# A cross-attention and quantized feed-forward kernel: a first pass over all batches, gate arithmetic on 128 partitions, decay exponents by one matmul of four heads, another order of attention and weight units

## The reference

```python
x = x + mlstm(layernorm(x), ctx, ctx, Wi, bi, Wf, bf, ln_scale)
x = x + ffn(layernorm(x), w_gate, w_up, w_down)
# mlstm, for each batch and head
log_f_cum = cumsum(log_sigmoid(fg)); log_D = tril(log_f_cum[s] - log_f_cum[t]) + ig[t]
D = exp(log_D - max_t log_D); C = (q @ k.T) / sqrt(32) * D
n = maximum(abs(C.sum(-1)), exp(-max_log_D)); h = (C / (n + EPS)) @ v
hn = (h - mean(h)) * rsqrt(var(h) + EPS) * ln_scale
# ffn: every operand quantized (_q_act to 3 mantissa bits, _q_w to 1, shared power of two per 32)
inter = silu(q_act(x) @ q_w(w_gate).T) * (q_act(x) @ q_w(w_up).T)
out = q_act(inter) @ q_w(w_down).T
```

## Time and profile before

| | |
|---|---|
| median of 3 runs | 626.4 us (624.54 to 626.63) |
| the profiled execution | 627.32 us |
| its span, first to last instruction | 625.5 us |
| mean granted TensorE clock | 0.837 |
| first feed-forward matmul (gate of tile 0) | at 419.9 us |
| first and last `c_mult` of the attention | 38.5 and 405.3 us |
| one round in the steady part (from one L935 to the next, 212.86 to 261.87 us) | 49 us |

### The profile page before, as it was taken

One profiled execution on the slowest core, in us unless ns is written; L12 is line 12 of the kernel. 1 busy time (PEld: TensorE's weight loads), 2 busy tenths in 40 slices (PEclk: granted clock), 3 DMA queues, 4 the chain that ended last, 5 costly groups with the idle time before them and its releaser, 6 DMA issues.

```text
span 625.5 us, 10355 instructions
## 1 busy us (share of the span) xinstructions
PE 500.4 (80%) x2944; PEld 324.3 (52%) x2992; DVE 516.3 (83%) x759; ACT 379.1 (61%) x739; POOL 381.2 (61%) x359
## 2 busy tenths in 40 slices
PE   1768689679789779867868768457999999999994
PEld 1356575566566557745646565343444444444441
DVE  1257899999999999999999999947788888888882
ACT  2487786787877867867867876632333443343342
POOL 5456677778668758848858758763334344444443
PEclk9977877787777875878866957757999999999999
DMA  5330313212302312302311301001011111111120
GB/s 129 136 102 1 102 35 103 101 35 103 101 34 101 101 34 101 101 34 94 103 38 47 121 1 34 18 1 50 1 44 58 34 51 49 34 59 41 34 67 34
DMA packets 25479, 38.48 MB, mean 62 GB/s; under 512 B 4848, under 2 KB 8944, under 8 KB 25456
## 3 DMA queue, kind: packets, MB, share of 16 engines
q1 hardware_dynamic: 25456, 38.21, 18.8%
HBM read 29.82 MB, written 8.39 MB: 61 GB/s over the span
## 4 chain that ended last, share of the span: by engine, by line
PE 40%; DVE 33%; issue 13%; ACT 8%; POOL 4%; DVEq 1%; DMA 1%; POOLq 0%; ACTq 0%; SPq 0%
PE psA L1335 7%; PE psA L1344 7%; PE psC L1362 5%; PE psA L1171 4%; PE psA L1145 4%; DVE wam L887 3%; PE psC L1204 3%; PE psC L1113 3%; DVE CT L959 3%; DVE f L935 3%; DVE wn L915 2%; POOL wn L598 2%; PE psB L1354 2%; ACT Dt L694 2%; PE psC L1195 2%
## 5 line engine op out<-in xcount | busy, mean ns | idle before, releaser
L598 POOL TENSOR_TENSOR wn<-wq,ps 128x1024 bf16<-128x1024 bf16 x32 | 61.1, 1911 | 109.7 <-DVE wq L1088 109.7
L1171 PE MATMUL psA<-vp,CT 128*128 128x33 f32 x512 | 83.5, 321 | 24.3 <-DVE CT L959 24.1
L1171 PEld LDWEIGHTS psA<-vp,CT 128*128 128x128 f32 x512 | 80.6, 243 | 29.6 <-issue 15.5
L1145 PE MATMUL psA<-qbd,kT 128*128 128x512 f32 x128 | 71.6, 711 | 0.4 <-issue 0.4
L694 ACT ACTIVATE Dt<-psB,gT 128x128 f32<-128x128 f32 x256 | 70.9, 376 | 0.2
L494 POOL TENSOR_TENSOR wq<-wn,ws 128x1024 bf16<-128x1024 bf16 x24 | 45.9, 1911 | 38.4 <-DVE wn L916 38.4
L844 ACT ACTIVATE wy<-psB 128x1024 bf16<-128x1024 bf16 x32 | 32.7, 1023 | 59.1 <-PE psB L1354 58.5
L501 POOL TENSOR_TENSOR wy<-wm,wy 128x1024 f32<-128x1024 f32 x24 | 63.2, 2632 | 0.9 <-ACT wm L676 0.9
L1335 PE MATMUL psA<-WgT,xqT 128*128 128x512 bf16 x241 | 61.6, 395 | 2.3 <-ACT WdT L687 1.5
L1362 PE MATMUL psC<-WdT,wy 128*128 128x512 bf16 x248 | 60.1, 379 | 2.9 <-ACT wy L844 2.4
L1344 PE MATMUL psA<-WuT,xqT 128*128 128x512 bf16 x255 | 62.0, 386 | 0.2 <-issue 0.2
(11 more groups left out here) (130 smaller groups left out, 1103.3 us busy)
## 6 DMA issues: line engine op xcount, KB each, us to landing
xt<-in_x_dram SPq DMA_DIRECT2D x8, 512.0 KB, 4.8
ct<-in_ctx_dram SPq DMA_DIRECT2D x8, 512.0 KB, 3.4
wraw<-in_L_ffn_w_gate_dram SPq DMA_DIRECT2D x8, 512.0 KB, 4.1
wraw<-in_L_ffn_w_up_dram SPq DMA_DIRECT2D x8, 512.0 KB, 4.8
wraw<-in_L_ffn_w_down_dram SPq DMA_DIRECT2D x8, 512.0 KB, 3.8
xr<-in_x_dram SPq DMA_DIRECT2D x16, 256.0 KB, 2.7
x_scratch<-x SPq DMA_DIRECT2D x16, 256.0 KB, 2.1
wm<-x_scratch SPq DMA_DIRECT2D x16, 256.0 KB, 2.7
```

The lines of the kernel that those rows point to most:

```text
L598: nc.gpsimd.tensor_tensor(blocks(pd[h][:, :]), blocks(pc[h][:, :]), spread(ps4[h][:, :], PB), ALU.mult).then_inc(pq_ready.sem, 1)
L1145: nc.tensor.matmul(psA[:, i4, :], kT[p][:, i4, c * P:(c + 1) * P], qbd[:, i4, :, :].rearrange("p j t -> p (j t)"), start=True, stop=True). ...
L1171: last = nc.tensor.matmul(psA[:, i4, j * VW:(j + 1) * VW], CT[n % 2][:, j * P:(j + 1) * P], vp[p][:, c, HPC * i4 + j, :], start=True, stop ...
```

## The change

- **First pass.** A loop of eight `pre_step`s does, per batch, the loads of x and context, their statistics, normalization, sixteen transposes into `qTa` and `kTa` (now kept for all batches), and one unit of `w_down`. The gates of all batches gather in one PSUM bank, tokens on partitions; then they are transposed once, so that the 16 heads of 8 batches stand on 128 partitions and the log-sigmoid, scans and splits run once. The results (the exponents as three bfloat16 parts each) go to DRAM and are fetched batch by batch (`load_decay` with eight DMAs, `load_carry` with four).
- **Decay exponents.** Both parts of the exponent (of the query and of the key position) are in one product: `statt` (32 rows) by `movt` (32 rows, 512 columns) after the mask matmul. `exps` is one exponential of 128x512 without a bias.
- **Scores.** No `qbd`: `qk` is sixteen products of 32 rows with 128 columns per chunk, straight from `kTa` and `qTa`. `inter` is sixteen products of 32 rows and 33 columns that go on adding in the PSUM banks of `heads`; the factor of the carry is multiplied into the query by `carry_q` on POOL. `combine` goes; `copy_h` copies both chunks.
- **Tail.** Both chunks of a batch at once, one batch late; `head_power` and the four small POOL operations become one `pow` over 128x32 on POOL.
- **Weight unit.** `round_const` is one ACT pass; `add_w` goes; `w_round` is two DVE operations of two SBUF inputs; the multiplication back (`w_back`) moves from POOL to DVE. Eight units lie in the first pass, two in each attention step.
- **Order.** A new list for each engine, below. SBUF tiles that are spent serve the second phase; its instructions are the same.

The new side of the diff, cut to what matters (12 blanks of indentation taken off; in the weight functions `w` counts the 24 units, `p` is the buffer):

```diff
+def load_decay(b, p):
+    rows = bass.ts(b, NH)
+    for c in range(NCH):
+        r = DROW * (2 * p + c)
+        t = slice(c * P, (c + 1) * P)
+        sp.dma_start(movt[r:r + SPLIT, :, :].rearrange("s j (i t) -> s (j i) t", t=P),
+                     gs_dram[0:SPLIT, rows, t]).then_inc(d_ld, 16)
+        for s in range(SPLIT):
+            k = r + SPLIT + HC * s
+            sp.dma_start(statt[k:k + HC, :, :],
+                         gs_dram[SPLIT + s, rows, t].rearrange("(j i) t -> i j t", i=HC)).then_inc(d_ld, 16)
...
+    nc.gpsimd.affine_select(out=mask[:, :, :], in_=mask[:, :, :], compare_op=ALU.is_ge, fill=NEG,
+                            base=0, pattern=[[0, HC], [1, P]],
+                            channel_multiplier=-1).then_inc(tables_ready, 1)
+    done = 0
+    for slot in range(2 * NCH):
+        for s in range(SPLIT):
+            if done:
+                gp.wait_ge(hot_step, done)
+            nc.gpsimd.affine_select(out=hot[:, :], in_=hot[:, :], compare_op=ALU.not_equal, fill=1.0,
+                                    base=-(DROW * slot + SPLIT + HC * s), pattern=[[-1, HC]],
+                                    channel_multiplier=1).then_inc(hot_step, 1)
+            done += 1
...
+def pre_step(b, p, n, first, last):
+    scale_w(b, p)
+    if not last:
+        x_rsqrt(b + 1)
...
+def head_rsqrt(b):
+    gp.wait_ge(hv_ready.sem, hv_ready.at(b, 1))
+    nc.gpsimd.tensor_tensor(sm[:, 4, :, :].rearrange("p c h -> p (c h)"),
+                            sm[:, 3, :, :].rearrange("p c h -> p (c h)"), mhalf[:, :],
+                            ALU.pow).then_inc(hr_ready.sem, 1)
...
+def residual(b):
+    hn = sq.rearrange("p c h d -> p c (h d)")
+    gp.wait_ge(hn_ready.sem, hn_ready.at(b, 1))
+    ch.link(nc.gpsimd.tensor_tensor(hn, hn, lns[:, :].unsqueeze(1).broadcast_to([P, NCH, E]), ALU.mult))
+    gp.wait_ge(xr_ld, 16 * b + 16)
+    gp.wait_ge(x1_st, 16 * b + 16)
+    gp.wait_ge(xn_ready.sem, xn_ready.at(b, 0))
+    settle(gp)
+    nc.gpsimd.tensor_tensor(x1, hn, xr, ALU.add).then_inc(x1_ready.sem, 1)
...
+def carry_q(b):
+    gp.wait_ge(g5b_ld, 16 * HPC * b + 16 * HPC)
+    gp.wait_ge(inter_done.sem, inter_done.at(b, 0))
+    settle(gp)
+    nc.gpsimd.tensor_tensor(qs[:, :, :], qTa[:, b, :, P:S], g5b[:, :, :], ALU.mult).then_inc(qs_ready.sem, 1)
...
+def step(b, p, n, first, last):
+    if not last:
+        scale_w(2 * b + B + 2, 0)
+    if not first:
+        head_rsqrt(b - 1)
+        residual(b - 1)
+        x1_rsqrt(b - 1)
+    if not last:
+        scale_w(2 * b + B + 3, 1)
         weigh(b + 1, 1 - p)
+        carry_q(b + 1)
+    if not first:
+        back_x(b - 1)
...
+def round_const(w, p):
+    act.wait_ge(pow_ready.sem, pow_ready.unit(w))
+    nc.scalar.activation(wm[p][:, :], wm[p][:, :], ACT.Identity, scale=W_SLOPE,
+                         bias=wbase[:, 0:1]).then_inc(m_ready.sem, 1)
...
+def pre_step(b, p, n, first, last):
+    copy_T(b, 0)
+    copy_T(b, 1)
+    if not last:
+        x_norm(b + 1, 1 - p)
+    round_const(b, p)
+    if not first:
+        evac_down(b - 1, b - 1)
...
+def exps(b, n):
+    act.wait_ge(c_ready.sem, c_ready.at(b, max(n - 1, 0)))
+    act.wait_ge(d_mm.sem, d_mm.at(b, n + 1))
+    nc.scalar.activation(Dt[n % 2][:, :], psB[n % 2][:, :], ACT.Exp).then_inc(d_exp.sem, 1)
...
+def step(b, p, n, first, last):
+    if not first:
+        square(b - 1)
+    exps(b, 0)
+    exps(b, 1)
+    if not last:
         copy_v(b + 1, 1 - p, 0)
+    exps(b, 2)
+    exps(b, 3)
+    evac_gate_up(2 * b + B + 1, 1, b)
+    if not last:
+        round_const(2 * b + B + 2, 0)
+    exps(b, 4)
+    copy_h(b, 0)
+    if not first:
+        x1_norm(b - 1)
+    exps(b, 5)
+    if not last:
         copy_v(b + 1, 1 - p, 1)
+    exps(b, 6)
+    if not last:
+        evac_gate_up(2 * b + B + 2, 0, b + 1)
+    exps(b, 7)
+    if not last:
         copy_state(b + 1)
+        round_const(2 * b + B + 3, 1)
+    copy_h(b, 1)
+    if not first:
+        evac_xq(b - 1)
...
+def w_round(w, p):
+    ve.wait_ge(m_ready.sem, m_ready.unit(w))
+    ch.link(nc.vector.scalar_tensor_tensor(out=wy[p][:, :], in0=wy[p][:, :], scalar=W_LOW, in1=wm[p][:, :],
+                                           op0=ALU.max, op1=ALU.add))
+    ve.wait_ge(wT_mm.sem, wT_mm.unit_before(w, 2))
+    nc.vector.scalar_tensor_tensor(out=wq[p][:, :], in0=wy[p][:, :], scalar=W_HIGH, in1=wm[p][:, :],
+                                   op0=ALU.min, op1=ALU.subtract).then_inc(wn_ready.sem, 1)
...
+def w_back(w, p):
+    ve.wait_ge(wn_ready.sem, wn_ready.unit(w))
+    nc.vector.tensor_tensor(blocks(wq[p][:, :]), blocks(wq[p][:, :]), spread(ws4[p][:, :], UB),
+                            ALU.mult).then_inc(wq_ready.sem, 1)
...
+def pre_step(b, p, n, first, last):
+    w_front(b, p, n)
+    if not first:
+        w_round(b - 1, 1 - p)
+    if not last:
+        x_stats(b + 1, *after(p, n))
+    if not first:
+        w_back(b - 1, 1 - p)
+    w_pow(b, p)
...
+def head_var(b):
+    n = hf[:, :, :, DH]
+    ve.wait_ge(h_ev.sem, h_ev.at(b, 2))
+    ch.tag(nc.vector.scalar_tensor_tensor(out=sm[:, 0], in0=n, scalar=-1.0, in1=n, op0=ALU.mult, op1=ALU.max))
+    ve.wait_ge(sq_ready.sem, sq_ready.at(b, 1))
     ch.wait()
+    low = gT[:, 0:NCH, bass.ts(b, NH)].rearrange("p c (j i) -> p c i j", i=HC)
+    ch.link(nc.vector.tensor_tensor(sm[:, 1].rearrange("p c (i j) -> p c i j", j=HPC),
+                                    sm[:, 0].rearrange("p c (i j) -> p c i j", j=HPC), low, ALU.max))
+    ch.link(nc.vector.tensor_scalar(sm[:, 1], sm[:, 1], EPS, D_MAX, ALU.add, ALU.min))
+    nc.vector.scalar_tensor_tensor(out=sm[:, 0], in0=sm[:, 1], scalar=EPS, in1=sm[:, 1],
+                                   op0=ALU.mult, op1=ALU.mult)
+    ch.link(nc.vector.reduce_sum(sm[:, 2], sq, AX.X))
+    nc.vector.scalar_tensor_tensor(out=sm[:, 3], in0=sm[:, 2], scalar=1.0 / DH, in1=sm[:, 0],
                                    op0=ALU.mult, op1=ALU.add).then_inc(hv_ready.sem, 1)
...
+def step(b, p, n, first, last):
+    if not last:
+        w_front(2 * b + B + 2, 0, b + B // 2 + 1)
+    if not first:
+        head_var(b - 1)
     c_mult(b, 0)
     c_mult(b, 1)
+    w_round(2 * b + B + 1, 1)
     c_mult(b, 2)
+    if not first:
+        head_norm(b - 1)
+    w_back(2 * b + B + 1, 1)
     c_mult(b, 3)
+    if not last:
+        w_pow(2 * b + B + 2, 0)
+    if not first:
+        x1_stats(b - 1)
     c_mult(b, 4)
+    if not last:
+        w_front(2 * b + B + 3, 1, b + B // 2 + 1)
     c_mult(b, 5)
+    if not last:
+        w_round(2 * b + B + 2, 0)
+    if not first:
+        x1_round(b - 1)
     c_mult(b, 6)
+    if not last:
+        w_back(2 * b + B + 2, 0)
     c_mult(b, 7)
+    if not last:
+        w_pow(2 * b + B + 3, 1)
...
+def pre_step(b, p, n, first, last):
+    transpose_q(b, p, first)
+    transpose_k(b, p, n, first)
+    if first:
+        gate_bias()
     else:
+        gates(b - 1)
+        w_transpose(b - 1, 1 - p, cols_order)
...
+def qk(b, c):
+    pe.wait_ge(h_ev.sem, h_ev.at(b, c))
+    settle(pe)
+    for i4 in range(HC):
+        for j in range(HPC):
+            r = slice(DH * j, DH * (j + 1))
+            last = nc.tensor.matmul(psA[:, j, i4 * P:(i4 + 1) * P], kTa[r, b, i4, c * P:(c + 1) * P],
+                                    qTa[r, b, i4, c * P:(c + 1) * P], start=True, stop=True)
+            if i4 == HC - 1:
+                last.then_inc(qk_done.sem, 1)
...
+def decay(b, p, n):
+    c, j = divmod(n, HPC)
+    if n == 0:
+        pe.wait_ge(d_ld, 16 * NCH * (1 + SPLIT) * b + 16 * NCH * (1 + SPLIT))
+    if not (isinstance(b, int) and b == 0 and n < 2):
+        pe.wait_ge(d_exp.sem, d_exp.at(b, n - 1))
+    r = slice(DROW * (2 * p + c), DROW * (2 * p + c + 1))
+    nc.tensor.matmul(psB[n % 2][:, :], identb[:, :], mask[:, :, :].rearrange("p i t -> p (i t)"),
+                     start=True, stop=False, skip_group_check=True)
+    nc.tensor.matmul(psB[n % 2][:, :], statt[r, j, :], movt[r, j, :], start=False, stop=True,
+                     skip_group_check=True).then_inc(d_mm.sem, 1)
...
+def inter(b):
+    pe.wait_ge(state_ev.sem, state_ev.at(b, 1))
+    pe.wait_ge(qs_ready.sem, qs_ready.at(b, 1))
+    for i4 in range(HC):
+        for j in range(HPC):
+            r = slice(DH * j, DH * (j + 1))
+            last = nc.tensor.matmul(psA[:, j, i4 * VW:(i4 + 1) * VW], qs[r, i4, :], Sst[r, i4, :],
+                                    start=False, stop=True, skip_group_check=True)
+    last.then_inc(inter_done.sem, 1)
...
+def step(b, p, n, first, last):
+    qk(b, 0)
     heads(b, p, 0)
+    decay(b, p, 2)
+    if not last:
+        centre(b + 1, 0)
     heads(b, p, 1)
+    decay(b, p, 3)
     heads(b, p, 2)
+    decay(b, p, 4)
+    if not first:
+        pe.wait_ge(xqT_ev.sem, xqT_ev.at(b - 1, 0))
+    w_transpose(2 * b + B + 1, 1, rows_order)
     heads(b, p, 3)
+    decay(b, p, 5)
+    qk(b, 1)
+    if not last:
+        centre(b + 1, 1)
     heads(b, p, 4)
+    decay(b, p, 6)
     heads(b, p, 5)
+    decay(b, p, 7)
+    if not last:
```

(88 more changed lines are left out.)

1345 lines of the change are left out of this document (548 added, 797 removed).

## The result

The changed kernel takes 685.61 us in the median of four runs (683.64 to 688.18) against 626.18 us (624.54 to 626.63): 1.096 times the time, 95% interval 1.091 to 1.100. Slower was forecast, but by 3.4% and not by 9.6%, and the time lies just above the range of 606 to 684 us.

A forecast was written before the change was run, and what follows sets the result against it. VectorE (95% busy) was taken to bound attention rounds, TensorE the feed-forward phase. After the change, 118 + 21 + 40.3 + 5 x 43.0 + 35.9 + 5.0 = 435, then 212: span 647, forecast 648 us, range 606 to 684.

The forecast's parts named there:

- back_x behind carry_q behind inter: Attention step, GpSimd: carry_q (1.27 us) waits for inter (2.0) to release qs, and back_x (1.91) stands behind carry_q.
- square behind evac_xq: Attention step, ScalarE: the square (1.1 us) stands behind evac_xq (1.02 us).
- exps(7) behind the copy behind w_back: End of an attention step: exps(7) waits for the unit's copy, which needs transposes after w_back; 2.4 us a step.
- the pow: head_rsqrt on GpSimd, 32 columns: 5.2 us from the slope per column, bounds 0.7 and 5.2, then releasing head_norm.
- rival 3: The pow holds VectorE, so w_round runs after it: 3.3 us more per step, 671 us; chance 0.10.
- The first c_mult: End of the first pass and gate arithmetic: forecast at 118 us against 38.5 before, bounds 105 and 150.
- Part B: Attention step from the end of head_norm to the last c_mult: a chain of 25.4 us, 0.8 of it hand-overs.
- step 0: First attention step, which has no tail: 21 us.
- Rival 2: TensorE decides: 666 us with row groups one after another, 716 at the lower clock as well; chance 0.12.
- Steps 2 to 6: Five full attention steps, forecast at 43.0 us each, with all TensorE and DMA work beside the chain.
- part A: Attention step from the previous batch's last c_mult to the end of its head_norm: one chain of 17.6 us.
- rival 1: Faster: the chain has slack and VectorE's own sum decides; steps of 36 us, 598 us; chance 0.22.

The follow-up runs named there:

- e14: The changed kernel with weighted scores and values of the head products in bf16 instead of fp32: 658.7 us.
- e5: The changed kernel with every mask product issued four times, 24 more long streams per attention step: 682.1 us.
- e4: The changed kernel with ten more 128x512 bf16 products after the inter-chunk product: 685.0 us.
- e6: The changed kernel with the next batch's first-chunk centring products and ScalarE's copy of them one head group later: 687.1 us.
- e7: The changed kernel with five order edits: back_x before carry_q, first unit's copy after exps(7), centring later, x1_round after c_mult(7), square straight behind copy_h: 635.8 us.
- e10: e7 with w_front of the second unit moved before c_mult(4): 624.7 us, ratio 1.000 to the kernel before.
- e15: e10 with weighted scores and values of the head products in bf16 instead of fp32: 601.9 us.

## Why the prediction was right in sign and wrong in size

Right was the reading that VectorE's 12 us per batch can't be had while the lists hand the work from engine to engine. Of the links named ahead these are in the trace: back_x behind carry_q behind inter, square behind evac_xq, exps(7) behind the copy behind w_back. One is not: head_norm was to be released by the pow, and it waits for c_mult(2) in front of it. The pow came at 5.43 us for 5.2 (so the slope of the earlier trace rows held over 32 columns). VectorE ran both rounding operations under it at 1.21 and 1.23 us, so rival 3 is out.

Two sums came out well in part by luck. The first c_mult came 1 us before its forecast: the last normalization ended at 81.9 us instead of 84.4, and the rest took 35.1 us instead of 33.7. Part B came within 0.1 us: from head_norm to the end of the residual sum it took 6.1 us for 6.6, w_round under GpSimd's products 3.6 for 3.0, and the end from w_back to c_mult(7) 3.6 for 2.8, with the transposes at the lower clock; the 0.8 us allowed for hand-overs covered the difference. The residual product took 3.27 us where the forecast had 2.34 behind w_back: it was started while w_back ran, and waited for it, as forecast.

The span came out 37.5 us above the 647 us worked out: 31 in the steps, 2 up to the first gate matmul, 5 in the feed-forward phase (the first back_p 19.7 us after the first gate matmul instead of 18.1, the rest not taken apart), less 1 in the first pass. The failed step is the price of TensorE in the attention steps: "All PE and DMA work of it [...] lies beside this chain", with heads, transposes and step 0 priced from rows at the higher clock. Rival 2 had the lower clock, at the wrong price (716; it had inter at 6.8 us, and it took 1.93) and with a chance that was too small. Steps 2 to 6, each 3.7 us above the forecast in the mean, make 18 of the 31. Step 3, which was 46.9 us long, shows where: its part A is 4.0 us above the forecast. First PE:

```profile
238.72 1.93 PE L1249 MATMUL psA<-Sst,qs 32*128 32x33 f32 x32
244.23 1.01 PE L1257 MATMUL psC<-identb,xc 128*128 128x128 bf16 x8 [3.57 <-POOL xc L629]
...
253.29 2.08 PE L1196 MATMUL psC<-cen,kTa 128*128 128x128 f32 x8
```

ScalarE:

```profile
255.40 0.60 ACT L749 ACTIVATE vp<-psC 128x512 f32<-128x512 f32 x1 [7.09 <-PE psC L1196]
255.89 0.59 ACT L774 ACTIVATE Dt<-psB 128x512 f32<-128x512 f32 x1
```

GpSimd:

```profile
240.95 1.26 POOL L624 TENSOR_TENSOR qs<-qTa,g5b 128x512 f32<-128x512 f32 x1 [14.39 <-issue]
242.18 1.91 POOL L629 TENSOR_TENSOR xc<-xc,xs 128x1024 bf16<-128x1024 bf16 x1
...
249.67 5.43 POOL L590 TENSOR_TENSOR sm<-sm,mhalf 128x32 f32<-128x32 f32 x1 [3.72 <-DVE sm L1009]
```

VectorE:

```profile
236.13 0.69 DVE L993 SCALAR_TENSOR_TENSOR CT<-psA,Dt 128x512 f32<-128x512 f32 x1 [2.93 <-ACT Dt L774]
...
247.57 0.22 DVE L1003 TENSOR_TENSOR sm<-sm,gT 128x32 f32<-128x32 f32 x1 [3.42 <-ACT early L789]
...
256.62 0.69 DVE L993 SCALAR_TENSOR_TENSOR CT<-psA,Dt 128x512 f32<-128x512 f32 x1 [3.17 <-ACT Dt L774]
257.23 1.22 DVE L1014 TENSOR_TENSOR early<-hf,sm 128x1024 f32<-128x1024 f32 x1
```

The last c_mult ends at 236.8 and head_norm at 258.45. Heads and inter end at 240.65, 0.9 us later than priced (at the lower clock, the 1.93 of inter itself is as forecast); the transposes take 1.01 instead of 0.5; three small operations of head_var after the square add 0.6 that the sum had left out, and the pow 0.2. The pow ends at 255.10, and head_norm still waits 2.1 us, because c_mult(2) in front of it waits for exps(2), that for ScalarE's copy, and that for centring products of 2.08 us at the lower clock. This last wait was not seen at all. 0.9, 0.5, 0.8 for these two and 2.1 are 4.3; 0.3 comes back in hand-overs that were fewer than allowed. Step 0 has no tail; its extra 9.0 us are not taken apart further than e14 does: heads in bf16 take 3.6 of them away.

e14 shows that TensorE's price is real: cheaper head products bring 27 us. That this is near the 31 that the steps lacked is no measure of the miss, since a bf16 group takes 0.30 us where the forecast itself had 0.97. e5 and e4 show that it isn't the clock alone, because raising it to 0.67 brought 3.5 us and to 0.60 nothing (with the cost of the streams in both). How the 31 us split between the clock and the order stays open: no run had the higher clock without added products. e6 shows that the new wait, taken away by itself, brings nothing: so the 2.1 us are part of this path, and yet no price of their own.

The prediction's larger omission is what its own list of waits could have shown: the order, not the change of algorithm, held 50 us (e7), and with w_front moved 61 us (e10). The 80 to 100 us that VectorE's sum promised can be had in part only: behind the order stands TensorE at 90% busy and 1.2 GHz (e10), and behind that a chain, through GpSimd as far as its waits show (e15, 35.6 us a step, about the 36 that rival 1 gave).

## What to carry to other kernels

When a change takes the busiest engine from 95% to 60%, ask which list then sets the step, and put long operations with slack (here x1_round, 3.9 us) behind the short ones that release other engines. A single wait taken away brought 6 us at most here; five together brought 50. Price every matmul at both clocks when the change takes long streams away from TensorE.
